# Relative-position attention: far value products in pairs every second step, six probability buffers, maxima respread

## The chip, the cores and the metric

One core of a Trainium2 chip runs the whole program. The metric is the device time of one execution in microseconds (us). Engines: TensorE (PE, matrix products; PEld is its weight load), VectorE (DVE), ScalarE (ACT), GpSimd (POOL), and SP, which issues DMA transfers.

## What is computed

A pre-norm transformer layer on x of 2 x 2048 x 256: attention with 16 heads of 16 and clipped relative positions (distance at most 64), then a feed-forward part with block-wise FP4 quantising (untouched here).

```python
dist = jnp.clip(idx[None, :] - idx[:, None], -R, R) + R          # R = 64
score = einsum('bhqd,bhkd->bhqk', q, k) + einsum('bhqd,qkd->bhqk', q, rel_emb_k[dist])
attn = softmax(score)
ctx = einsum('bhqk,bhkd->bhqd', attn, v) + einsum('bhqk,qkd->bhqd', attn, rel_emb_v[dist])
```

## The kernel before

`transformer_layer` runs projections, attention and the feed-forward part one after the other. Attention works in 32 iterations: 8 groups g (2 batch entries x 4 groups of 4 heads) times 4 query blocks qb of 512 queries. An iteration goes over all 2048 keys in 16 steps (STEPS). A step is one tile of 128 keys against 512 queries for 4 heads. Steps 0 and 1 hold the band of keys near the diagonal (`near_half`, L835), steps 2 to 15 the far ones (`far_half`, L859); steps 2 to 4 mix pieces of several tiles (`pieces`, L1137).

A step has two units, each of two heads. A unit is written by TensorE in two halves into two banks of psS. psS has four banks, so it holds two units: a unit's first half waits until ScalarE has read the unit two places before (`unit_free`, L831). ScalarE (`iteration`, L999) takes the exponential of each unit, 128 x 1024, into `band` or `probs`. `probs` (L596) has 4 unit buffers, which is two steps; before the first exp of a far step ScalarE waits on the semaphore pv_done until the value products that read those buffers are over (L1014 to L1017).

The order on TensorE is written out by hand: `ORDER` (L549) has one string per step, and the loop at L912 issues one piece of work per letter:

- S: half a unit of scores (L867; in steps 0 and 1 L847 and L854).
- M: one maximum product (L756), a 128 x 512 tile of scores of the coming query block into one of two banks of psA, from which VectorE takes the row maximum (`take`, L1044, L1047). Of an iteration's 64 products, each waits until the maximum two places before is taken (L754). They belong to the next iteration up to step 12, and from step 13 (ASTEPS) on to the one after it.
- V: in steps 3 to 15 the value products of the step before (`far_values`, L773 to L782): for each piece four products of 32 (or 17) columns of the array, one per head, from `probs` into psC. In step 0 it is those of step 15 of the previous iteration; in step 2 the band's own (`band_values`, L872).
- R: the relative products of the next block (L769), in steps 4 to 7; they use psS as a unit does, and ScalarE copies them to rel_scores (`copy_rel`, L990), VectorE reduces them (`rel_maxima`, L1049).
- P: positions (`positions`, L884, L896), 64 columns wide. F: `fold_positions` (L902, L909), 32 columns wide, into psC.
- D and B: denominators and their turning back (L789, L799) for the iteration before. T: the turn of the negated maxima (`turn_maxima`, L784), which wait for VectorE's minus maxima (L1055) in step 13; ScalarE copies them (L985), POOL cuts them in three parts (L699), SP stores them as query rows (L641), and the first near scores of the next iteration wait for that (L850).

VectorE (`iteration`, L1076) walks the same steps: `RATE[step]`, the count of M in a step's string, sets how many maxima it takes there, with the row maxima of R behind the third take of steps 5 to 8, the masks of positions ahead of steps 10 and 12, the reciprocal ahead of step 2 and the product behind the first take of step 3.

The semaphore pv_done is raised once per far value step, 14 in an iteration (VALUE_STEPS), and by 2 at the start; `copy_context` (L978) waits for all of an iteration's. ScalarE does it behind the second exp of the next iteration. In the last iteration (`ends`) there are no M, R and T, and the value products left over come behind the loop (L947).

Of the kernel before, what the change touches and what calls it, by code (L numbers as in the profile page):

```python
# [27 lines left out]
ACT = mybir.ActivationFunctionType  # L28
AX = mybir.AxisListType

P = 128
# [7 lines left out]
NQ = 512  # L39
# [463 lines left out]
class Consts:  # L503
# [20 lines left out]
STEPS = 16  # L524
# [10 lines left out]
VALUE_STEPS = STEPS - BAND_STEPS  # L535
# [11 lines left out]
PSTEP = 8  # L547

ORDER = (  # L549
    "SMSMVMSMSMMM", "SMSMMSMMSMMD", "SMSMVMMBSSM", "SMSSMSVM",  # L550
    "SMSSMSMVRM", "SMSSMSVRM", "SMSSMSMVRM", "SMSSMSVRM",
    "SMSSMSMVMP", "SMSSMSMVMP", "SMSSMSMVFMP", "SMSSMSMVMP",
    "SMSSMSVMF", "SMSSMSVMT", "SMSSMSVM", "SMSSMSVM",
)
RATE = tuple(x.count("M") for x in ORDER)
ASTEPS = 13
AHEAD = sum(RATE[ASTEPS:])
assert sum(RATE) == ROUND


def place(n, ends=False):

    return n if ends else n + min(max(n // 2 - RSTEP, 0), RUNITS)


def rel_place(k):

    return 2 * (RSTEP + k) + 2 + k


def first_of(it):

    return it * SEQ + RUNITS


def attention(nc, c, dr, io):
    with ExitStack() as ctx:
        def sb(name, shape, dt=F32):
            return ctx.enter_context(nc.sbuf_tensor(name, shape, dt))
# [13 lines left out]
        keys, qs, vals, keys_in, q_in = io.keys, io.qs, io.vals, io.keys_in, io.q_in  # L593
        rel = sb("rel_scores", [P, APAIRS, DREL])
        near = sb("rel_near", [P, APAIRS, 2, P])
        probs = sb("probs", [P, 4, 2, NQ])  # L596
        band = sb("band_probs", [P, 2, HG, CH, P])
        relp = sb("rel_products", [P, 2, NQ])
        amax = sb("amax", [P, APAIRS, APER])
# [139 lines left out]
        def _(pe):  # L739
# [33 lines left out]
            def far_values(g, qb, step, ends=False):  # L773

                pe.wait_ge(unit_done, first_of(g * QB + qb) + place(2 * step + 1, ends) + 1 + 2)
                for o, tile, q0, k in pieces(qb, step):
                    for h in range(HG):
                        n = 2 * step + h // 2
                        v = values_of(g, tile, h)
                        ins = t.matmul(psC[32 * h:32 * h + v.shape[1], q0:q0 + k], v,  # L780
                                       probs[:, n % 4, h % 2, o:o + k], start=False, stop=False, skip_group_check=True)
                ins.then_inc(pv_done, 1)  # L782

            def turn_maxima(m):  # L784
# [22 lines left out]
            def iteration(g, par, qb, gp, first=False, last=False):  # L807
                it = g * QB + qb
                base = first_of(it)
                ends = last and qb == QB - 1  # L810
                g1, par1, qb1 = (g + 1, 1 - par, 0) if qb == QB - 1 else (g, par, qb + 1)
                g2, par2, qb2 = (g, par, qb + 2) if qb < 2 else (g + 1, 1 - par, qb - 2)
                qp = (qb - 1) % QB

                todo = [] if ends else [(qb1, x) for x in maxima(g1, par1, qb1)][AHEAD:]
                ahead = [] if last and qb >= QB - 2 else [(qb2, x) for x in maxima(g2, par2, qb2)][:AHEAD]

# [94 lines left out]
                for step in range(STEPS):  # L912
                    if step == ASTEPS:
                        start_ahead()
                    score = near_half if step < BAND_STEPS else far_half
                    half = 0
                    for kind in ORDER[step]:
                        if kind == "M":
                            some(1)
                        elif kind == "S":  # L920
                            score(2 * step + half // 2, half % 2)
                            half += 1
                        elif kind == "R":
                            if not ends:
                                k = step - RSTEP
                                rel_products(it + 1, qb1, k, base + rel_place(k))
                        elif kind == "P":
                            positions(*divmod(step - PSTEP, 2))
                        elif kind == "F":
                            fold_positions((step - PSTEP) // 2 - 1)  # L930
                        elif kind == "D":
                            if not first:
                                denominators(it - 1)
                        elif kind == "B":
                            if not first:
                                turn_back(it - 1)
                        elif kind == "T":
                            if not ends:
                                turn_maxima(it + 1)
                        elif step == 0:  # L940
                            if not first:
                                far_values(gp, qp, STEPS - 1)
                        elif step == 2:
                            band_values()
                        else:
                            far_values(g, qb, step - 1, ends)
                if ends:  # L947
                    far_values(g, qb, STEPS - 1, ends)
                    denominators(it)
                    turn_back(it)  # L950

            pe.sem_inc(pv_done, 2)
            pe.wait_ge(keys_in, KDMAS * 16)
            pe.wait_ge(q_in[0], 6 * 16)
            for k in range(RUNITS):
# [3 lines left out]
            pe.wait_ge(q_in[1], 6 * 16)  # L959
            for item in list(maxima(0, 0, 1))[:AHEAD]:  # L960
                max_product(1, item)
# [12 lines left out]
        @block.scalar  # L974
        def _(act):
            a = nc.scalar

            def copy_context(it):  # L978


                act.wait_ge(pv_done, (it + 1) * VALUE_STEPS + 2)
                act.wait_ge(norm_ready, it + 1)
                a.copy(ctxs[:], psC[:]).then_inc(ctx_copied, 1)

            def copy_shift(m):  # L985

                act.wait_ge(turn_ready, m + 1)
                a.copy(sres[:, 0, :], psM[0:2 * APAIRS, 0:P]).then_inc(shift_copied, 1)  # L988

            def copy_rel(m, k, at):  # L990

                if k == 0:
                    act.wait_ge(skew_out, m * 16)
                act.wait_ge(rel_max, m * RUNITS)
                act.wait_ge(unit_ready, at + 1)
                a.copy(rel[:, 4 * k:4 * k + 4, :].rearrange("p (b x) r -> p b (x r)", b=2),  # L996
                       psS[:, 2 * (k % 2):2 * (k % 2) + 2, :]).then_inc(unit_done, 1)

            def iteration(g, qb, first=False, last=False):  # L999
                it = g * QB + qb  # L1000
                base = first_of(it)
                ends = last and qb == QB - 1
                for n in range(UNITS):
                    if n == 2 * ASTEPS + 2 and not ends:
                        copy_shift(it + 1)
                    if n == 2 and not first:
                        copy_context(it - 1)
                    act.wait_ge(unit_ready, base + place(n, ends) + 1)
                    src = psS[:, 2 * (place(n, ends) % 2):2 * (place(n, ends) % 2) + 2, :]
                    if n < 2 * BAND_STEPS:  # L1010
                        e, c2 = divmod(n, 2)
                        ins = a.activation(band[:, e, 2 * c2:2 * c2 + 2].rearrange("p h u q -> p h (u q)"), src, ACT.Exp)  # L1012
                    else:
                        if n % 2 == 0:  # L1014

                            act.wait_ge(pv_done, it * VALUE_STEPS + n // 2 - BAND_STEPS + 1)
                        ins = a.activation(probs[:, n % 4], src, ACT.Exp)  # L1017
                    ins.then_inc(unit_done, 1)
                    if n % 2 == 1 and RSTEP <= n // 2 < RSTEP + RUNITS and not ends:
                        k = n // 2 - RSTEP  # L1020
                        copy_rel(it + 1, k, base + rel_place(k))
                if ends:
                    copy_context(it)

            act.sem_inc(unit_done, 2)
            act.sem_inc(ctx_copied, 1)
            for k in range(RUNITS):
                copy_rel(0, k, k)
            copy_shift(0)
            iteration(0, 0, first=True)  # L1030
            for g in range(GRP - 1):
                for qb in range(1, QB):
                    iteration(g, qb)
                if g < GRP - 2:
                    iteration(g + 1, 0)
            for qb in range(QB):
                iteration(GRP - 1, qb, last=True)
# [3 lines left out]
        def _(dve):  # L1041
# [34 lines left out]
            def iteration(g, qb, first=False, last=False):  # L1076
# [3 lines left out]
                g1, qb1 = (g + 1, 0) if qb == QB - 1 else (g, qb + 1)  # L1080
                todo = [] if ends else [((it + 1) * ROUND, n) for n in range(AHEAD, ROUND)]
                ahead = [] if last and qb >= QB - 2 else [((it + 2) * ROUND, n) for n in range(AHEAD)]

# [7 lines left out]
                for step in range(STEPS):  # L1091
                    if step == ASTEPS:
                        assert not todo
# [30 lines left out]
            dve.wait_ge(negm_ready, 1)  # L1124
            for n in range(AHEAD):
                take(ROUND, n)
# [599 lines left out]
```

## Time and profile before

| | us |
|---|---|
| median of 3 runs (2590.91 to 2592.51) | 2591.05 |
| the profiled execution's own time | 2594.04 |
| its span, first to last instruction | 2592.3 |
| TensorE busy (share of the span) | 2382.4 (92%) |
| VectorE busy | 1930.2 (74%) |
| ScalarE busy | 1361.9 (53%) |
| POOL busy | 606.9 (23%) |

Mean granted clock of TensorE 0.972 (1.00 is the higher of its two levels, 2.4 GHz). Busy times overlap, and the ends of matmuls are modelled: a 512-column product counts 0.38 us while the next one can start after 0.22. Attention lies between about 180 and 2146 us of the span.

### The profile page before, as it was taken

The page shows a single profiled execution, that of the slowest core. Times are in us where ns is not written, and L with a number is a line of the kernel's source. Part 1 is how long each engine was busy: PE and PEld are TensorE (multiplying, and loading weights), DVE is VectorE, ACT ScalarE, POOL GpSimd, SP SyncE. Part 2 cuts the span into 40 slices and gives each one's busy share as a digit, 9 for nine tenths or more (in the row PEclk, how much of TensorE's full clock was granted, in tenths as well). Part 3 has the DMA queues.
Part 4 walks back from the last instruction along what each step waited for, and adds up shares of the span by engine and source line. Part 5 has one row for each costly group of instructions (what it writes and reads, how often), then busy time and mean ns, then how long its engine had stood idle before and what let it go on. Part 6 is the DMA issues. An engine that isn't in the chain of part 4 may idle for free. (4 is left out here: it accounts for less than half of the span.)

```text
span 2592.3 us, 47776 instructions
## 1 busy us (share of the span) xinstructions
PE 2382.4 (92%) x19372; PEld 1179.2 (45%) x19372; DVE 1930.2 (74%) x3509; ACT 1361.9 (53%) x1572; POOL 606.9 (23%) x361
## 2 busy tenths in 40 slices
PE   7879999999999999999999999999999993899997
PEld 3424444444444444444444444444444442566665
DVE  6587777777777777777777777777777726899997
ACT  3405555565555555555555555555555561334442
POOL 5402222222222222222222222222222220011111
PEclk9959999999999999999999999999999996999998
DMA  5723323332333333323332332333222221111110
GB/s 159 184 75 86 85 77 85 88 85 76 85 84 96 93 89 101 99 78 85 85 85 82 93 85 77 85 88 85 76 77 77 71 70 54 43 40 49 49 40 27
DMA packets 275656, 210.35 MB, mean 81 GB/s; under 512 B 17058, under 2 KB 266628, under 8 KB 275332
## 3 DMA queue, kind: packets, MB, share of 16 engines
q1 hardware_dynamic: 274308, 203.37, 28.5%
q0 software_dynamic: 1152, 4.19, 0.6%
q8 instruction: 144, 2.36, 0.4%
q14 instruction: 52, 0.43, 0.1%
HBM read 113.35 MB, written 93.34 MB: 80 GB/s over the span
## 5 line engine op out<-in xcount | busy, mean ns | idle before, releaser
L1047 DVE TENSOR_REDUCE amax<-psA 128x1 f32<-128x512 f32 x2048 | 1327.7, 686 | 494.3 <-PE psA L756 485.9
L1017 ACT ACTIVATE probs<-psS 128x1024 f32<-128x1024 f32 x896 | 885.0, 1023 | 483.5 <-PE psS L867 483.0
L756 PE MATMUL psA<-keys,queries 96*128 96x512 bf16 x2048 | 789.0, 392 | 43.8 <-DVE amax L1047 43.6
L867 PE MATMUL psS<-queries,keys 102*128 102x512 bf16 (+7 forms) x2176 | 632.5, 343 | 44.7 <-ACT rel_scores L996 36.8
L780 PE MATMUL psC<-probs,vals 128*32 128x512 f32 (+7 forms) x4352 | 475.0, 524 | 0.6 <-ACT probs L1017 0.6
L756 PEld LDWEIGHTS psA<-keys,queries 96*128 96x128 bf16 x2048 | 196.4, 97 | 500.5 <-DVE amax L1047 439.2
L717 POOL TENSOR_TENSOR band_probs<-band_probs,side 128x2048 f32<-128x2048 f32 x64 | 288.6, 4533 | 559.5 <-PE psC L880 559.5
L867 PEld LDWEIGHTS psS<-queries,keys 102*128 102x128 bf16 (+1 forms) x2176 | 203.4, 99 | 282.0 <-ACT rel_scores L996 98.1
L1012 ACT ACTIVATE band_probs<-psS 128x1024 f32<-128x1024 f32 x128 | 131.1, 1024 | 224.1 <-PE psS L854 224.1
L996 ACT COPY rel_scores<-psS 128x1024 f32<-128x1024 f32 x128 | 129.3, 1012 | 106.9 <-PE psS L769 106.9
L780 PEld LDWEIGHTS psC<-probs,vals 128*32 128x32 f32 (+1 forms) x4352 | 89.1, 102 | 174.0 <-issue 166.5
L1342 PE MATMUL psG<-w_gate_up_T,f_xqT 128*128 128x352 f32 x512 | 162.8, 473 | 0.9 <-ACT f_xqT L1396 0.9
L847 PE MATMUL psS<-ident,rel_near 128*128 128x128 f32 x1024 | 156.0, 274 | 0.0
L723 POOL TENSOR_TENSOR band_probs<-band_probs 128x2048 f32<-128x2048 f32 x32 | 145.0, 4531 | 5.7 <-POOL band_probs L721 2.9
L847 PEld LDWEIGHTS psS<-ident,rel_near 128*128 128x128 f32 x1024 | 129.6, 142 | 21.4 <-issue 2.0
L703 POOL CAST shift<-shift_res 32x128 bf16<-32x128 f32 x32 | 9.0, 281 | 520.0 <-ACT shift_res L988 520.0
L1281 POOL TENSOR_TENSOR f_hq<-f_h_grid,f_h_scale 128x704 f32<-128x704 f32 x32 | 44.4, 1387 | 355.2 <-DVE f_h_grid L1510 355.2
L1342 PEld LDWEIGHTS psG<-w_gate_up_T,f_xqT 128*128 128x128 f32 x512 | 97.7, 196 | 51.8 <-issue 4.9
L854 PE MATMUL psS<-queries,keys 102*128 102x128 bf16 (+1 forms) x1024 | 100.6, 220 | 6.7 <-DMA queries<-shift 6.7
L697 POOL MEMSET rel_near<- 128x256 f32 x16 | 5.1, 318 | 410.3 <-DMA rel_near<-rel_skew 410.3
L1374 PE MATMUL psD<-w_down_T,f_hqT 128*128 128x256 f32 (+1 forms) x384 | 96.5, 394 | 2.0 <-ACT f_hqT L1402 2.0
L1052 DVE TENSOR_REDUCE rel_max_of<-rel_scores 128x4 f32<-128x512 f32 x128 | 86.6, 676 | 10.2 <-ACT rel_scores L996 10.2
(162 smaller groups left out, 2054.2 us busy)
## 6 DMA issues: line engine op xcount, KB each, us to landing
rel_skew<-rel_scores SPq DMA_DIRECT2D x32, 2048.0 KB, 7.5
rel_near<-rel_skew SPq DMA_DIRECT2D x64, 1024.0 KB, 8.1
keys<-k_ring SPq DMA_DIRECT2D x48, 256.0 KB, 5.7
queries<-q_parts SPq DMA_DIRECT2D x192, 64.0 KB, 2.4
ctx_d<-rden SPq DMA_DIRECT2D x32, 256.0 KB, 2.3
ctx_in<-ctx_d SPq DMA_DIRECT2D x32, 256.0 KB, 2.7
q_parts<-parts SPq DMA_DIRECT2D x16, 384.0 KB, 2.9
k_ring<-parts SPq DMA_DIRECT2D x12, 384.0 KB, 3.1
```

The lines of the kernel that those rows point to most:

```text
L717: p.tensor_mul(both, both, c.side[:, e, None, :].broadcast_to([P, APAIRS, P])).then_inc(side_cut, 1)
L723: p.tensor_add(band[:, 0].rearrange("p h u q -> p (h u q)"), band[:, 0].rearrange("p h u q -> p (h u q)"), band[:, 1].rearrange("p h u q - ...
L756: t.matmul(psA[:, n % 2, :], qs[0:NR, qb, h, u * P:(u + 1) * P], keys[0:NR, par, h, c0:c0 + NQ], start=True, stop=True).then_inc(max_ready, 1)
L780: ins = t.matmul(psC[32 * h:32 * h + v.shape[1], q0:q0 + k], v, probs[:, n % 4, h % 2, o:o + k], start=False, stop=False, skip_group_check ...
L847: t.matmul(bank[:, u * P:(u + 1) * P], near[:, h * CH + u, e, :], c.ident[:], start=(u == 0), stop=False, is_transpose=True, skip_group_ch ...
L854: ins = t.matmul(bank[:, u * P:(u + 1) * P], keys[0:nr, par, h, c0:c0 + P], qs[0:nr, qb, h, u * P:(u + 1) * P], start=False, stop=(u == CH ...
L867: ins = t.matmul(bank[:, o:o + k], keys[0:nr, par, h, c0:c0 + P], qs[0:nr, qb, h, q0:q0 + k], start=True, stop=True, skip_group_check=True)
L996: a.copy(rel[:, 4 * k:4 * k + 4, :].rearrange("p (b x) r -> p b (x r)", b=2), psS[:, 2 * (k % 2):2 * (k % 2) + 2, :]).then_inc(unit_done, 1)
L1012: ins = a.activation(band[:, e, 2 * c2:2 * c2 + 2].rearrange("p h u q -> p h (u q)"), src, ACT.Exp)
L1017: ins = a.activation(probs[:, n % 4], src, ACT.Exp)
L1047: v.reduce_max(amax[:, pair, k:k + 1], psA[:, n % 2, :], AX.X).then_inc(max_taken, 1)
L1342: ins = t.matmul(psG[:, half, 0:GU], xqT[:, k, cc, :], wgu[:, cc, half * GU:(half + 1) * GU], start=(cc == 0), stop=(cc == 1))
```

## The change

`ORDER` is written anew. The value products of two far steps stand together in every even step but step 2, which keeps the band's: step s runs those of s-2 and s-1, and step 0 those of steps 14 and 15 of the previous iteration. Odd steps have none. The maxima per step go from 7 7 5 3 4 3 4 3 4 4 4 4 3 3 3 3 to 6 4 4 3 5 3 5 3 5 3 5 3 5 3 4 3, 64 in all as before, with the last three steps holding 9 before and 10 now. `probs` gets 6 unit buffers (three steps), the waits on pv_done count from 3 in place of 2, and `far_values` finds its buffers modulo 6. F of step 12 moves from behind an M to directly behind the couple; T still ends step 13.

```diff
--- before.py
+++ after.py
@@ -547,13 +547,15 @@
 PSTEP = 8
 
 ORDER = (
-    "SMSMVMSMSMMM", "SMSMMSMMSMMD", "SMSMVMMBSSM", "SMSSMSVM",
-    "SMSSMSMVRM", "SMSSMSVRM", "SMSSMSMVRM", "SMSSMSVRM",
-    "SMSSMSMVMP", "SMSSMSMVMP", "SMSSMSMVFMP", "SMSSMSMVMP",
-    "SMSSMSVMF", "SMSSMSVMT", "SMSSMSVM", "SMSSMSVM",
+    "SMSMVVMSMSMM", "SMSMSMSMD", "SMSMVMBSSM", "SMSSMSM",
+    "SMSMSMSVVMRM", "SMSSMSRM", "SMSMSMSVVMRM", "SMSSMSRM",
+    "SMSMSMSVVMPM", "SMSSMSMP", "SMSMSMSVVFMPM", "SMSSMSMP",
+    "SMSMSMSVVFMM", "SMSSMSMT", "SMSMSSMVVM", "SMSSMSM",
 )
 RATE = tuple(x.count("M") for x in ORDER)
 ASTEPS = 13
+
+PSTEPS = 3
 AHEAD = sum(RATE[ASTEPS:])
 assert sum(RATE) == ROUND
 
@@ -593,7 +595,7 @@
         keys, qs, vals, keys_in, q_in = io.keys, io.qs, io.vals, io.keys_in, io.q_in
         rel = sb("rel_scores", [P, APAIRS, DREL])
         near = sb("rel_near", [P, APAIRS, 2, P])
-        probs = sb("probs", [P, 4, 2, NQ])
+        probs = sb("probs", [P, 2 * PSTEPS, 2, NQ])
         band = sb("band_probs", [P, 2, HG, CH, P])
         relp = sb("rel_products", [P, 2, NQ])
         amax = sb("amax", [P, APAIRS, APER])
@@ -778,7 +780,7 @@
                         n = 2 * step + h // 2
                         v = values_of(g, tile, h)
                         ins = t.matmul(psC[32 * h:32 * h + v.shape[1], q0:q0 + k], v,
-                                       probs[:, n % 4, h % 2, o:o + k], start=False, stop=False, skip_group_check=True)
+                                       probs[:, n % (2 * PSTEPS), h % 2, o:o + k], start=False, stop=False, skip_group_check=True)
                 ins.then_inc(pv_done, 1)
 
             def turn_maxima(m):
@@ -913,7 +915,7 @@
                     if step == ASTEPS:
                         start_ahead()
                     score = near_half if step < BAND_STEPS else far_half
-                    half = 0
+                    half, values = 0, 0
                     for kind in ORDER[step]:
                         if kind == "M":
                             some(1)
@@ -937,19 +939,21 @@
                         elif kind == "T":
                             if not ends:
                                 turn_maxima(it + 1)
-                        elif step == 0:
-                            if not first:
-                                far_values(gp, qp, STEPS - 1)
                         elif step == 2:
                             band_values()
                         else:
-                            far_values(g, qb, step - 1, ends)
+                            back, values = 2 - values, values + 1
+                            if step:
+                                far_values(g, qb, step - back, ends)
+                            elif not first:
+                                far_values(gp, qp, STEPS - back)
                 if ends:
-                    far_values(g, qb, STEPS - 1, ends)
+                    for back in (2, 1):
+                        far_values(g, qb, STEPS - back, ends)
                     denominators(it)
                     turn_back(it)
 
-            pe.sem_inc(pv_done, 2)
+            pe.sem_inc(pv_done, PSTEPS)
             pe.wait_ge(keys_in, KDMAS * 16)
             pe.wait_ge(q_in[0], 6 * 16)
             for k in range(RUNITS):
@@ -978,7 +982,7 @@
             def copy_context(it):
 
 
-                act.wait_ge(pv_done, (it + 1) * VALUE_STEPS + 2)
+                act.wait_ge(pv_done, (it + 1) * VALUE_STEPS + PSTEPS)
                 act.wait_ge(norm_ready, it + 1)
                 a.copy(ctxs[:], psC[:]).then_inc(ctx_copied, 1)
 
@@ -1014,7 +1018,7 @@
                         if n % 2 == 0:
 
                             act.wait_ge(pv_done, it * VALUE_STEPS + n // 2 - BAND_STEPS + 1)
-                        ins = a.activation(probs[:, n % 4], src, ACT.Exp)
+                        ins = a.activation(probs[:, n % (2 * PSTEPS)], src, ACT.Exp)
                     ins.then_inc(unit_done, 1)
                     if n % 2 == 1 and RSTEP <= n // 2 < RSTEP + RUNITS and not ends:
                         k = n // 2 - RSTEP
```

## Rows read from the trace of the kernel before

**Rows 1.** Windows: attention, last iteration, feed-forward (span; PE PEld DVE ACT POOL busy; clock; DMA; GB/s).

```profile
254.00:1063.00 809.00, 775.38 (x7191) 356.63 (x7191) 603.49 (x986) 472.42 (x499) 199.35 (x103) 1.00 0.32 87
2101.27:2142.81 41.54, 38.99 (x451) 17.56 (x449) 2.33 (x4) 31.18 (x33) 14.08 (x4) 1.00 0.03 7
2146.00:2592.00 446.00, 360.23 (x1452) 254.81 (x1452) 382.21 (x908) 156.11 (x266) 50.54 (x36) 0.92 0.14 44
```

**Rows 2.** Windows: one iteration, steps 6-7, steps 12-13, steps 0-1.

```profile
1001.31:1063.01 61.70, 59.17 (x551) 27.11 (x550) 45.96 (x76) 36.14 (x39) 14.95 (x7) 1.00 0.34 89
1015.53:1023.17 7.64, 6.85 (x40) 2.24 (x39) 5.65 (x9) 5.91 (x6) 1.68 (x1) 1.00 0.01 2
1039.02:1045.07 6.05, 6.05 (x51) 2.01 (x48) 4.46 (x10) 3.82 (x4) 0.00 (x0) 1.00 0.28 69
1050.38:1062.04 11.66, 10.96 (x95) 7.71 (x94) 9.45 (x15) 4.67 (x6) 0.00 (x0) 1.00 0.43 81
```

**Rows 3.** Waits of TensorE in that iteration: total us, times, longest.

```profile
PE psS L867 <- ACT rel_scores L996: 1.2, 4, 0.3
PE psA L756 <- DVE amax L1047: 1.1, 4, 0.5
```

**Rows 4.** Timeline, TensorE: start, length, line, operation, count [idle before <-releaser].

```profile
1016.63 0.39 PE L867 MATMUL psS<-queries,keys 102*128 102x512 bf16 x1 [0.29 <-ACT rel_scores L996]
...
1017.08 0.38 PE L867 MATMUL psS<-queries,keys 102*128 102x512 bf16 x1
1017.67 0.39 PE L756 MATMUL psA<-keys,queries 96*128 96x512 bf16 x1 [0.21 <-DVE amax L1047]
1017.99 1.07 PE L780 MATMUL psC<-probs,vals 128*32 128x512 f32 x8
1018.99 0.61 PE L769 MATMUL psS<-rel_rows,queries 96*128 96x256 bf16 x4
1019.43 0.38 PE L756 MATMUL psA<-keys,queries 96*128 96x512 bf16 x1
...
1042.77 0.60 PE L867 MATMUL psS<-queries,keys 99*128 99x512 bf16 x2
```

**Rows 5.** Timeline, ScalarE and VectorE, at the same times.

```profile
1015.57 1.01 ACT L996 COPY rel_scores<-psS 128x1024 f32<-128x1024 f32 x1 [0.58 <-PE psS L769]
1016.47 2.04 ACT L1017 ACTIVATE probs<-psS 128x1024 f32<-128x1024 f32 x2
1019.69 1.01 ACT L996 COPY rel_scores<-psS 128x1024 f32<-128x1024 f32 x1 [1.17 <-PE psS L769]
...
1043.19 1.02 ACT L1017 ACTIVATE probs<-psS 128x1024 f32<-128x1024 f32 x1 [1.36 <-PE psS L867]
...
1016.93 1.88 DVE L1047 TENSOR_REDUCE amax<-psA 128x1 f32<-128x512 f32 x3
...
1019.85 0.69 DVE L1047 TENSOR_REDUCE amax<-psA 128x1 f32<-128x512 f32 x1 [0.45 <-PE psA L756]
```

**Rows 6.** Timeline, TensorE: value step, fold, maximum, positions, scores.

```profile
1033.00 1.06 PE L780 MATMUL psC<-probs,vals 128*32 128x512 f32 x8
1033.88 0.62 PE L909 MATMUL psC<-rel_products,fold 128*32 128x128 f32 x16
1034.43 0.39 PE L756 MATMUL psA<-keys,queries 96*128 96x512 bf16 x1
1034.75 0.69 PE L896 MATMUL psM<-band_probs,tv 128*64 128x64 f32 x16
1035.37 0.39 PE L867 MATMUL psS<-queries,keys 102*128 102x512 bf16 x1
```

**Rows 7.** Timeline, VectorE: minus maxima in step 13.

```profile
1042.58 0.22 DVE L1059 TENSOR_REDUCE negm<-amax 128x16 f32<-128x64 f32 x1
...
1043.13 1.29 DVE L1047 TENSOR_REDUCE amax<-psA 128x1 f32<-128x512 f32 x2
```

**Rows 8.** Groups by line, TensorE: near scores behind the shifts' transfer.

```profile
L854 PE MATMUL psS<-queries,keys 102*128 102x128 bf16 (+1 forms) x1024 | 100.6, 220 | 6.7 <-DMA queries<-shift 6.7
```

## The prediction

> **What bounds the kernel now.** The page ranks the engines: TensorE is the fullest, VectorE next, ScalarE behind. By stage, attention runs with TensorE 96% busy and the granted clock at 1.00, the feed-forward part behind it at 81% [rows 1]. The change touches attention alone, 32 iterations, so the question is what ends last there. A steady iteration lasts 61.70 us, and the same view cut at the starts of steps gives it in pairs of steps [rows 2]. TensorE sets the pace, but not by its work alone: it waits for ScalarE to free a score buffer (psS holds two units) and for VectorE to free one of two maximum buffers (psA) [rows 3]. These rows understate the waits, since a matmul counts 0.38 us as busy while the next one starts 0.22 behind it. So I count from start to start.
>
> **Slots**, start to start, in us: a half unit of scores (S) and a maximum product (M) 0.22 each (0.45 for both), a relative product (R) 0.45, a far value step (V) ahead of a full-width product 1.00, an M ahead of V 0.32 [rows 4]; V ahead of the fold (F) 0.88, F ahead of M 0.55, the position products (P) ahead of S 0.62 [rows 6]. Entering the narrow (32- and 64-column) products thus costs 0.10 and leaving them 0.11; net of that V is 0.87, F 0.45, P 0.50. Summed over an iteration, work and switches are 56.8 us; the other 4.9 are waits.
>
> **What the change removes.** Fourteen far value steps, of which each stands alone, become seven couples: seven entries and exits go, 7 x 0.21 = 1.5 us. The F of step 12 joins a couple, another 0.21. That is 1.7 us an iteration, all on TensorE's path. V beside V isn't in this trace. Its nearest row is V beside F, both 32 columns wide; the bounds are 0.87 (no exit) and 1.00 (an exit all the same). I take 0.87.
> The counts are otherwise the same: 64 M, 14 V, 4 R, the same transfers, exps and maxima; SP's and POOL's orders aren't touched. Two more buffers of probabilities cost 8 KB a partition and no instruction. ScalarE's wait before the first exp of step s now asks for the values of step s-3 where it asked for those of s-2. In the new order they stand in step s-2 or s-1 at the latest, so no exp waits for them and nothing queues behind that wait; without the third pair of buffers it would bind.
> T, the turn of the maxima, still ends step 13. The scores behind its transfer wait 6.7 us in all now, 0.2 a round [rows 8]; the way from T to them grows by 0.4 by the table below, so about half of that wait, 0.1, goes.
>
> **What it adds: waits.** Two rules come out of the rows [rows 4, 5]. An exp starts 0.42 after the second half of its unit, lasts 1.02, and the buffer is free 0.06 later; the copy of R starts 0.70 after R, and the next exp 0.90 after that copy. A maximum is taken 0.42 after its M started, takes follow each other by 0.60, one lasts 0.69, and the M two places on may go 0.06 later. Worked through the new order from the first S of step 5, at 0: R of step 5 at 2.02, M 2.47, S of step 6 at 3.04 (0.35 of it behind exp 11), M 3.26, S 3.48, M 3.70, S 4.05 (0.13 behind the copy of R). VectorE still has the last maximum and the row maxima of step 5 ahead, so its takes for step 6 start at 4.08 and 4.68, and the third M waits 0.56, to 4.83. S 5.05, V 5.37, V 6.24, M 7.22, R 7.44, M 7.89, and step 7 starts at 8.11. There the second unit waits 0.39 for the copy of R, and R 0.26 for an exp. Step 8 starts at 11.15. The pair 6-7 lasts 8.11, against 7.64 before [rows 2]: its waits grow from 1.3 to 1.75, the switch gives 0.21 back, and one M came in. While both Vs run, 1.85 us, ScalarE and VectorE empty their two buffers and stand idle; between couples six units and eight maxima come as a burst.
> Steps 12 and 13: step 12 now ends V V F M M. Those two takes and the three operations of the minus maxima, 0.55 [rows 7], stand in a row on VectorE; the first M of step 13 waits 0.50 for a take, the third 0.70. Nothing waited here before.
> The same rules over all pairs, as work + switches + waits:
> 2-3: before 7.1 + 0.6 + 0.4 = 8.1, after 6.0 + 0.4 + 0.4 = 6.8 (a V went to step 4);
> 4-5: before 5.9 + 0.4 + 0.7 = 7.0, after 6.15 + 0.2 + 1.6 = 8.0;
> 6-7: before 7.6, after 8.1;
> 8-9: before 6.3 + 0.85 + 0.8 = 7.9, after 6.3 + 0.6 + 1.15 = 8.1;
> 10-11: before 6.7 + 0.85 + 0.2 = 7.8, after 6.7 + 0.6 + 0.6 = 7.9;
> 12-13: before 5.4 + 0.6 + 0 = 6.0, after 5.8 + 0.2 + 1.6 = 7.7;
> 14-15: before 4.8 + 0.4 + 0.1 = 5.3, after 5.0 + 0.2 + 0.4 = 5.7;
> 0-1: before 10.1 + 0.2 + 1.3 = 11.5, after 10.1 + 0.2 + 0.2 = 10.5 (four Ms fewer, one V more, and the Ms there wait up to 0.5 now [rows 3]).
> Before comes to 61.3, against 61.70, and 7.6, 6.0 and 11.5 against 7.64, 6.05 and 11.66 [rows 2]. After comes to 62.8. Waits grow by 3.1, switches shrink by 1.7: **+1.44 an iteration**. Moving one input at a time (the spacing of takes by 0.01, a latency by 0.03, a slot by 0.005, the exit by 0.03) moves that between 1.2 and 1.6.
> The last iteration has no maxima and no R. Its steps hold four S, V and P, and the new order puts eight S ahead of V V, through two buffers that empty in 2 x 1.02 a step. By the same rules such a pair grows by 0.8, and with the last couple outside the loop some 6 come on top of 41.5 [rows 1].
> **Sum:** 30 x (1.44 - 0.11) = 40, the last iteration 6, the first and the one before the last about 0: +46. The profiled execution took 2594.04 (span 2592.3), the median of the runs is 2591.05, 3 us lower; 2594 + 46 = 2640 there, and **2637 us** on the median.
>
> The Trainium skill, page "TensorEngine Tiling" (Performance Considerations, PSUM Bottleneck), states that tiling speeds TensorE up and leaves the emptying of PSUM as it was, which then can become the bottleneck. This speaks against the change, and the trace agrees in that the waits named above are for exactly that; the page gives no figure for it.
>
> **Rivals.**
> *Only the switches count* (0.07). The waits stay at 4.9 and an iteration falls to 60.0: 31 x 1.7 = 53 less, 2538 us. For it: ScalarE and VectorE are busy 36 and 46 of 61.7 us [rows 2]. Against: even so TensorE waits for both today, two buffers deep, and a couple doubles the stretch which they must bridge. The Trainium skill, page "TensorEngine Tiling" (Key Properties), states that changing the tiling mode drains the engine; the 0.10 and 0.11 agree, and by that rule alone the result would be this one.
> *Waits grow, but less* (0.13), by 1.0 to 2.2 an iteration, as bursts overlap better than the account has it: 31 x (1.0 - 1.7) = -22 to 31 x (2.2 - 1.7) + 4 = +19, so 2569 to 2610.
> *The clock falls* (0.05). TensorE's idle share in attention grows; the part behind, at 81%, shows a granted clock of 0.92 [rows 1]. If 2% of it went in attention, 31 x 1.25 = 39 more, 2676.
> *The wait for buffers binds* (0.02). If the first exp of a step needed the couple beside it, each couple would cost one exp, 7 x 1.02 x 31 = 220 more, 2857. The counts, as reckoned above, exclude it.
> My own forecast, 2610 to 2656, has the remaining 0.73.
>
> **How the numbers follow.** A measurement of this kernel tells 0.2%, 5 us, from no change. Slower by more: my forecast, the clock, the wait, and half of the second rival, 0.86. Within it 0.03. Faster: the first rival and the rest of the second, 0.11. The range leaves out the first rival, the faster part of the second and the two high ones: 2604 to 2656.
>
> **What would show it.** Right: steps 6-7 at 8.1, 12-13 at 7.7 with two waits for maxima in step 13, 2-3 at 6.8; V to V at 0.87; idle time before M about doubled, before S up by a third; no exp behind a V; the last iteration near 47. Wrong: the waits before M and S at their old size, V to V at 1.00, or a granted clock under 1.00 in attention.

## Result and the profile after

The changed kernel takes 2631.92 us (median of 4 runs, 2630.7 to 2634.69), the kernel before 2591.78 us beside it: 40 us more, a ratio of 1.0154 with a 95% interval of 1.0136 to 1.0171. The forecast was 2637 us, 46 more than before.

First the page of the changed kernel, busy times and the granted clock:

```profile
PE 2370.5 (90%) x19372; PEld 1178.0 (45%) x19372; DVE 1919.3 (73%) x3509; ACT 1368.1 (52%) x1572; POOL 606.5 (23%) x361
...
PEclk9959999999999999999999999999999996999999
```

TensorE is busy 12 us less than before, though the program is 40 us longer. The work shrank (the entries into narrow products and the exits from them), the idle time grew. The granted clock in attention is 1.00, as it was.

Windows of the changed kernel: attention, then one iteration cut at the starts of its steps (2-3, 4-5 and so on to 14-15, then 0-1), with the columns of [rows 1]:

```profile
254.00:1063.00 809.00, 757.23 (x7074) 347.64 (x7072) 586.48 (x967) 468.85 (x491) 199.20 (x103) 1.00 0.32 86
1013.06:1019.88 6.82, 6.59 (x121) 4.34 (x121) 4.09 (x8) 3.20 (x5) 3.69 (x1) 1.00 0.01 2
1019.88:1028.18 8.30, 7.42 (x61) 2.93 (x61) 5.88 (x11) 6.04 (x7) 8.12 (x3) 1.00 0.10 32
1028.18:1036.30 8.12, 7.13 (x49) 2.50 (x49) 6.31 (x11) 5.91 (x7) 1.73 (x1) 1.00 0.00 0
1036.30:1044.12 7.82, 7.33 (x64) 2.73 (x64) 6.48 (x11) 4.52 (x5) 0.00 (x0) 1.00 0.77 262
1044.12:1052.06 7.94, 7.74 (x84) 3.22 (x80) 5.57 (x10) 3.99 (x5) 0.00 (x0) 1.00 0.66 166
1052.06:1059.74 7.68, 6.52 (x54) 2.23 (x50) 5.46 (x12) 3.92 (x5) 0.00 (x0) 1.00 0.45 112
1059.74:1065.58 5.84, 5.84 (x33) 1.44 (x31) 4.35 (x8) 3.52 (x6) 1.40 (x4) 1.00 0.02 4
1065.58:1075.97 10.39, 10.39 (x100) 7.76 (x100) 7.41 (x12) 5.25 (x6) 0.00 (x0) 1.00 0.48 90
```

In attention TensorE is busy 93.6% (757 of 809), 95.8% before [rows 1], with the clock still at 1.00. In the kernel before, the windows of steps 4-5 and 8-9, which [rows 2] doesn't have, are:

```profile
1008.46:1015.53 7.07, 6.76 (x61) 3.04 (x60) 4.46 (x7) 4.89 (x5) 6.89 (x2) 1.00 0.12 37
1023.17:1031.22 8.05, 7.55 (x66) 2.71 (x64) 6.82 (x11) 4.89 (x5) 0.00 (x0) 1.00 0.75 256
```

Cut by pairs, in us, with the forecast beside them:

| steps | before | changed | forecast |
|---|---|---|---|
| 2-3 | 8.11 | 6.82 | 6.8 |
| 4-5 | 7.07 | 8.30 | 8.0 |
| 6-7 | 7.64 | 8.12 | 8.1 |
| 8-9 | 8.05 | 7.82 | 8.1 |
| 10-11 | 7.80 | 7.94 | 7.9 |
| 12-13 | 6.05 | 7.68 | 7.7 |
| 14-15 | 5.31 | 5.84 | 5.7 |
| 0-1 | 11.66 | 10.39 | 10.5 |
| sum | 61.69 | 62.91 | 62.8 |

Cut from one band value step (in step 2) to the next, the twenty-nine inner iterations differ by 35.3 us in all, 1.22 each. The last two add 6.5. The first one became 2.6 us shorter: its steps 0 and 1, which hold no value step of an earlier iteration and now four Ms fewer, fell from 19.7 to 16.3, and the stretch from its band value step to the next grew by 0.8. That makes 39.2 us for the 32 iterations. What stands ahead of them came out 0.9 longer and what stands behind, in the same code, 3.4 shorter in this pair of executions, so the two spans differ by 36.7 and the medians by 40.

Waits of TensorE in that iteration of the changed kernel (against [rows 3]):

```profile
PE psA L758 <- DVE amax L1051: 2.7, 7, 0.6
PE psS L869 <- ACT probs L1021: 0.6, 3, 0.2
PE psS L869 <- ACT rel_scores L1000: 0.4, 2, 0.2
```

The waits behind VectorE went from 4 to 7 and from 1.1 to 2.7 us. By these rows those for ScalarE did not grow. The same view over the stretch 254 to 1063 us, thirteen iterations:

```profile
PE psA L758 <- DVE amax L1051: 35.4, 91, 0.6
PE psS L869 <- ACT probs L1021: 8.0, 39, 0.2
PE psS L869 <- ACT rel_scores L1000: 5.8, 26, 0.5
```

Behind VectorE it is 35.4 us here and 15.2 in the kernel before, whose rows for this stretch stand with the experiments below.

The timeline of TensorE and of VectorE through step 6 of the changed kernel (against [rows 4, 5]):

```profile
1028.41 0.38 PE L758 MATMUL psA<-keys,queries 96*128 96x512 bf16 x1
1028.63 0.38 PE L869 MATMUL psS<-queries,keys 102*128 102x512 bf16 x1
1028.85 0.38 PE L758 MATMUL psA<-keys,queries 96*128 96x512 bf16 x1
1029.09 0.39 PE L869 MATMUL psS<-queries,keys 102*128 102x512 bf16 x1
1029.97 0.39 PE L758 MATMUL psA<-keys,queries 96*128 96x512 bf16 x1 [0.50 <-DVE amax L1051]
1030.20 0.38 PE L869 MATMUL psS<-queries,keys 102*128 102x512 bf16 x1
1030.51 1.93 PE L782 MATMUL psC<-probs,vals 128*32 128x384 f32 x24
1032.37 0.39 PE L758 MATMUL psA<-keys,queries 96*128 96x512 bf16 x1
...
1028.64 0.67 DVE L1056 TENSOR_REDUCE rel_max_of<-rel_scores 128x4 f32<-128x512 f32 x1
1029.23 1.88 DVE L1051 TENSOR_REDUCE amax<-psA 128x1 f32<-128x512 f32 x3
1031.03 0.67 DVE L1056 TENSOR_REDUCE rel_max_of<-rel_scores 128x4 f32<-128x512 f32 x1
1032.80 1.94 DVE L1051 TENSOR_REDUCE amax<-psA 128x1 f32<-128x512 f32 x3 [1.09 <-PE psA L758]
```

The third M starts at 1029.97. It follows an S of 1029.09, so without a wait it would have stood at 1029.31: it is 0.66 us late, of which the row shows 0.50 as idle time. VectorE took the row maxima of R at 1028.64 and so reached the first maximum of this step, whose M had started at 1028.41, only at 1029.23. That take ends at 1029.92. Then the couple runs from 1030.51 to the M at 1032.37, 1.86 us, and VectorE has nothing to do from 1031.70 to 1032.80, an idle time of 1.09.

Step 12 and 13 of the changed kernel, TensorE and VectorE:

```profile
1056.36 0.60 PE L758 MATMUL psA<-keys,queries 96*128 96x512 bf16 x2
...
1057.53 0.39 PE L758 MATMUL psA<-keys,queries 96*128 96x512 bf16 x1 [0.35 <-DVE amax L1051]
...
1059.40 0.39 PE L758 MATMUL psA<-keys,queries 96*128 96x512 bf16 x1 [0.61 <-DVE amax L1051]
1059.63 0.27 PE L789 MATMUL psM<-ident,negm 128*32 128x128 f32 x1
1059.74 0.38 PE L869 MATMUL psS<-queries,keys 99*128 99x512 bf16 x1
...
1056.78 1.29 DVE L1051 TENSOR_REDUCE amax<-psA 128x1 f32<-128x512 f32 x2 [2.12 <-PE psA L758]
1058.11 0.22 DVE L1063 TENSOR_REDUCE negm<-amax 128x16 f32<-128x64 f32 x1
...
1058.65 1.89 DVE L1051 TENSOR_REDUCE amax<-psA 128x1 f32<-128x512 f32 x3
```

Two Ms stand at 1056.36 (one row), their two takes at 1056.78, and the minus maxima behind them until the next take at 1058.65. The M of 1057.53 waited for a take and the M of 1059.40 for the next but one. In the kernel before, VectorE passed here with TensorE never idle (6.05 of 6.05 us busy [rows 2]).

### The profile page after: what moved, and what is told of

Read it like the earlier page. It is cut to its first block and busy times, and to the rows that moved or that the text cites. A ratio compares the mean times of both kernels' runs of the same rounds, so it can differ in the third digit from the quotient of the medians.

```text
span 2629.0 us, 47776 instructions
## 1 busy us (share of the span) xinstructions
PE 2370.5 (90%) x19372; PEld 1178.0 (45%) x19372; DVE 1919.3 (73%) x3509; ACT 1368.1 (52%) x1572; POOL 606.5 (23%) x361
## 5 line engine op out<-in xcount | busy, mean ns | idle before, releaser
L1051 DVE TENSOR_REDUCE amax<-psA 128x1 f32<-128x512 f32 x2048 | 1313.9, 685 | 539.9 <-PE psA L758 535.0
L1021 ACT ACTIVATE probs<-psS 128x1024 f32<-128x1024 f32 x896 | 894.9, 1023 | 569.5 <-PE psS L869 568.0
L869 PE MATMUL psS<-queries,keys 102*128 102x512 bf16 (+7 forms) x2176 | 648.9, 344 | 37.5 <-ACT probs L1021 23.8
L782 PE MATMUL psC<-probs,vals 128*32 128x512 f32 (+7 forms) x4352 | 430.4, 521 | 0.6 <-ACT probs L1021 0.6
L782 PEld LDWEIGHTS psC<-probs,vals 128*32 128x32 f32 (+1 forms) x4352 | 110.3, 103 | 208.9 <-issue 131.5
L849 PE MATMUL psS<-ident,rel_near 128*128 128x128 f32 x1024 | 157.1, 276 | 0.7 <-ACT probs L1021 0.7
L849 PEld LDWEIGHTS psS<-ident,rel_near 128*128 128x128 f32 x1024 | 126.7, 142 | 28.2 <-ACT probs L1021 9.9
```

The lines of the kernel that those rows point to most:

```text
L849: t.matmul(bank[:, u * P:(u + 1) * P], near[:, h * CH + u, e, :], c.ident[:], start=(u == 0), stop=False, is_transpose=True, skip_group_ch ...
L869: ins = t.matmul(bank[:, o:o + k], keys[0:nr, par, h, c0:c0 + P], qs[0:nr, qb, h, q0:q0 + k], start=True, stop=True, skip_group_check=True)
L1021: ins = a.activation(probs[:, n % (2 * PSTEPS)], src, ACT.Exp)
L1051: v.reduce_max(amax[:, pair, k:k + 1], psA[:, n % 2, :], AX.X).then_inc(max_taken, 1)
```

## The experiments

The readings below rest on the time between starts, as in the prediction. For one steady iteration of each trace (the eleventh) the table gives its length from one band value step to the next and the number of changes between full-width and narrow products (the one product of T, which shows no such cost, is left out). "Late" is what lies between two starts beyond the usual spacing of the same two kinds of product, from 0.04 us up, put down to the piece that started late; the usual spacing is taken low in the range of all traces, so these sums are good to about 0.2 us. Near scores are those of steps 0 and 1.

| kernel | iteration, us | changes of width | late far S and R | late M | late near scores |
|---|---|---|---|---|---|
| before | 61.69 | 42 | 2.2 | 2.6 | 0.1 |
| changed | 62.90 | 26 | 2.4 | 5.3 | 0.2 |
| couples alone (e2) | 63.01 | 28 | 3.3 | 4.0 | 0.5 |
| maxima alone (e3) | 62.09 | 40 | 1.2 | 4.4 | 0 |
| changed, none ending step 12 (e4) | 62.83 | 26 | 2.5 | 4.8 | 0.4 |
| before, short takes (e5) | 59.29 | 42 | 2.2 | 0.2 | 0.2 |
| changed, short takes (e6) | 58.71 | 26 | 3.0 | 0 | 0.7 |
| before, light (e7) | 58.87 | 42 | 1.8 | 0.2 | 0.2 |
| changed, light (e8) | 56.35 | 26 | 1.4 | 0 | 0.2 |
| single, reordered (e9) | 57.21 | 36 | 0 | 1.0 | 0 |
| couples, reordered (e10) | 57.48 | 32 | 0.2 | 1.3 | 0 |
| halves together (e11) | 61.10 | 42 | 0 | 4.4 | 0 |
| single, reordered again (e12) | 56.96 | 34 | 0.1 | 0.6 | 0 |

The theory: the couples save 1.7 us of switches an iteration and lose more in waits, because both reading engines work from two buffers each and run dry while a couple runs. The rivals: the new spread of the maxima does the harm, not the couples; V beside V saves nothing; the third pair of buffers costs something.

### The buffers alone

```diff
-        probs = sb("probs", [P, 4, 2, NQ])
+        probs = sb("probs", [P, 6, 2, NQ])
...
-                                       probs[:, n % 4, h % 2, o:o + k], ...
+                                       probs[:, n % 6, h % 2, o:o + k], ...
...
-            pe.sem_inc(pv_done, 2)
+            pe.sem_inc(pv_done, 3)
```

> The order of before, with probabilities of three steps held in place of two and the wait on pv_done counted accordingly. My theory: the third pair of buffers does nothing by itself, since no exp waits for a value step in the order of before: 2592 us, within 3. Rival (the larger buffer or the shifted wait costs or gains something of its own): more than 5 us off.

Measured: 2592.71 us, ratio 1.0002 (0.9993 to 1.0011). The buffers and the shifted wait are worth nothing either way in the order of before. The couples were not run with four buffers, so that they need the third pair stays the prediction's argument.

### The couples alone and the maxima alone

Couples, with before's counts of maxima:

```diff
...
-    "SMSSMSMVRM", "SMSSMSVRM", "SMSSMSMVRM", "SMSSMSVRM",
-    "SMSSMSMVMP", "SMSSMSMVMP", "SMSSMSMVFMP", "SMSSMSMVMP",
+    "SMSSMSMVVRM", "SMSSMSRM", "SMSSMSMVVRM", "SMSSMSRM",
+    "SMSSMSMVVMP", "SMSSMSMMP", "SMSSMSMVVFMP", "SMSSMSMMP",
...
```

> Couples and six buffers as changed, but as many maxima in each step as before (7 7 5 3 4 3 4 3 4 4 4 4 3 3 3 3). My theory: the couples themselves bring the waits, because scores and maxima come as a burst between them; by the two rules an iteration takes 62.7 us against 61.4 for before's order, so 30 x 1.3 and some 4 in the last iteration: 2635 us. Rival (the new spread of the maxima is the fault, and the couples pay): the waits stay as before and an iteration loses 1.7 us of switches: 2540 us.

Measured: 2636.58 us, ratio 1.0169 (1.0154 to 1.0185), 44 us above the kernel before beside it, where the whole change adds 40.

Single value steps, with the changed counts of maxima:

```diff
...
-    "SMSSMSMVRM", "SMSSMSVRM", "SMSSMSMVRM", "SMSSMSVRM",
+    "SMSMSMSVMRM", "SMSSMSVRM", "SMSMSMSVMRM", "SMSSMSVRM",
...
-    "SMSSMSVMF", "SMSSMSVMT", "SMSSMSVM", "SMSSMSVM",
+    "SMSMSMSVFMM", "SMSSMSVMT", "SMSMSSMVM", "SMSSMSVM",
...
```

> Value steps stand alone as before, four buffers, but the maxima are spread as in the change (6 4 4 3 5 3 5 3 5 3 5 3 5 3 4 3, two of them behind V in step 12). My theory: 61.8 us an iteration against 61.4, most of it in step 13: 2604 us. Rival (the spread is the fault): its whole growth of waits, 3.1 us an iteration, is here: 2685 us. Rival (the spread does nothing): 2592 us.

Measured: 2603.92 us, ratio 1.0038 (1.0025 to 1.0052). Each alone is slower than before, by 44 and by 11 us, and together they are 40: the new spread costs alone and helps the couples a little. The waits of TensorE over the same stretch, 254 to 1063 us, show which wait each brings. The kernel before:

```profile
PE psS L867 <- ACT rel_scores L996: 15.6, 52, 0.6
PE psA L756 <- DVE amax L1047: 15.2, 54, 0.5
PE psS L867 <- ACT probs L1017: 3.0, 13, 0.2
```

Couples alone:

```profile
PE psA L758 <- DVE amax L1051: 20.8, 65, 0.5
PE psS L869 <- ACT rel_scores L1000: 8.1, 26, 0.6
PE psS L869 <- ACT probs L1021: 8.0, 39, 0.2
```

Maxima alone:

```profile
PE psA L756 <- DVE amax L1047: 24.9, 65, 0.6
PE psS L867 <- ACT rel_scores L996: 5.8, 26, 0.5
PE psS L867 <- ACT probs L1017: 3.0, 13, 0.2
```

By these rows the couples bring the waits behind exps (3.0 to 8.0) and halve those behind the copy of R; both parts lengthen those for maxima. But idle time hides up to 0.16 us of each wait. From start to start the couples alone make far S and R 1.1 us an iteration later (2.2 to 3.3) and M 1.4 (2.6 to 4.0): they starve TensorE through both readers. The spread does its harm in M alone (2.6 to 4.4), while far S and R come 1.0 sooner.

### The maxima that end step 12

```diff
-    "SMSMVVMSMSMM", "SMSMSMSMD", "SMSMVMBSSM", "SMSSMSM",
+    "SMSMVVMSMSMMM", "SMSMSMMSMD", "SMSMVMBSSM", "SMSSMSM",
...
-    "SMSMSMSVVFMM", "SMSSMSMT", "SMSMSSMVVM", "SMSSMSM",
+    "SMSMSMSVVF", "SMSSMSMT", "SMSMSSMVVM", "SMSSMSM",
```

> The changed kernel with the two maxima behind V V F in step 12 moved to steps 0 and 1. The waits of 0.50 and 0.70 us in step 13 must go. My theory: they are partly paid elsewhere, since the scores then come sooner than ScalarE empties and the maxima wait in steps 0 and 1: 62.5 us an iteration in place of 62.76, so 8 us off the changed kernel, 2624 us. Rival (each wait is worth its own length): 1.2 x 30 = 36 off, 2596 us.

Measured: 2629.02 us, ratio to before 1.0142 (1.0126 to 1.0157), 3 to 4 us under the changed kernel where 8 were expected. Two Ms of step 13 that had been late by 0.5 and 0.8 us are late by 0.15 and 0.05. In their place an M of step 1 is 0.66 late, the S behind T 0.14 and the first near scores 0.19, and the inner iterations are 0.17 shorter on the mean. A wait's length is not its price.

### VectorE's part, then both engines' part

These four kernels leave part of the work out, to see what is paid for it. First VectorE reads 16 of the 512 columns of each maximum:

```diff
-                v.reduce_max(amax[:, pair, k:k + 1], psA[:, n % 2, :], AX.X).then_inc(max_taken, 1)
+                v.reduce_max(amax[:, pair, k:k + 1], psA[:, n % 2, 0:16], AX.X).then_inc(max_taken, 1)
```

> The order of before; VectorE takes each maximum over 16 of the 512 columns only (the rest of that reduction is left out), so that hardly anything waits for it. By the two rules an iteration falls from 61.4 to 59.2 us: 2592 - 31 x 2.2 = 2524 us. If waits for VectorE were hidden anyway: 2592.

Measured: 2497.47 us.

> The changed order, maxima taken over 16 of 512 columns as in the run beside it. By the two rules 58.8 us an iteration in place of 62.8, so the couples come out even or just ahead of the order of before under the same cut: 2632 - 31 x 3.9 = 2511 us, 5 to 15 under the run beside it. The waits for ScalarE remain (3.8 us an iteration against 2.3). Rival (the loss of the change doesn't come through VectorE): it stays 40 above the run beside it, 2565 us.

Measured: 2484.8 us (two runs of each, 2.4 us to either side here). Both fell further than expected by some 26 us, of which 20 lie ahead of the first band value step: the first round of maxima, which nothing covers, waits for its takes, and that step stands at 180 us where it was at 200. The order between the two is what counts: with VectorE's waits gone the changed order is 13 us ahead, where it was 40 behind. So waits for maxima make 53 us of the difference between the two orders. ScalarE still takes most of the gain: late far S and R stand at 3.0 in the changed order and at 2.2 in the other, late near scores at 0.7 and 0.2.

For the second pair each far exp is cut to 128 of its 1024 columns as well, and the buffers are zeroed once at the start:

```diff
-                        ins = a.activation(probs[:, n % 4], src, ACT.Exp)
+                        ins = a.activation(probs[:, n % 4, :, 0:64], psS[:, 2 * (place(n, ends) % 2):2 * (place(n, ends) % 2) + 2, 0:64], ACT.Exp)
...
+            v.memset(probs[:], 0.0).then_inc(probs_zero, 1)
```

> The order of before; maxima over 16 of 512 columns, and each far exp over 128 of its 1024 columns (the rest is left out; the buffers are zeroed once at the start). Waits for both engines nearly gone: 58.8 us an iteration, 2512 us.

Measured: 2489.84 us, 22 under the expected 2512, again mostly by the stretch ahead (186 us where 200 stood).

> The changed order with the same two cuts. With the waits gone the switches alone are left, and the change must win: 1.7 us of switches an iteration, and up to 0.6 of remaining waits for the copy of R: 56.4 to 57.1 us, so 53 to 73 us under the run beside it. Rival (V beside V costs as much as V alone): no gain, the two runs within 5 us.

Measured: 2413.99 us, 76 under the run beside it, 3 more than the highest value expected. This is the change's gain laid bare: 2.52 us an iteration, of which shorter remaining waits make 0.6 and 16 changes of width fewer the rest, some 1.85, or 0.115 each where the forecast had 0.106. From the pair with short takes to this one the changed order's lead grew from 13 to 76 us: in this order of cutting, 53 us pass through the maxima and 63 through the far exps. The timeline of TensorE in the light changed kernel, one couple with its neighbours:

```profile
1046.03 0.38 PE L869 MATMUL psS<-queries,keys 99*128 99x512 bf16 x1
1046.34 1.93 PE L782 MATMUL psC<-probs,vals 128*32 128x384 f32 x24
1048.20 0.39 PE L758 MATMUL psA<-keys,queries 96*128 96x512 bf16 x1
```

S to V is 0.31, the two Vs to the M behind them 1.86. A lone V with a full-width product behind it takes 1.00 [rows 4], so the second V adds 0.86. The rival that V beside V costs as much as V alone is out.

### Another order

The couples are one way to lower what TensorE spends; the waits, 4.9 us an iteration before, are the larger item. First only the score halves were moved together, from step 3 on:

```diff
...
-    "SMSSMSMVRM", "SMSSMSVRM", "SMSSMSMVRM", "SMSSMSVRM",
+    "MSSMSSMVRM", "MSSMSSVRM", "MSSMSSMVRM", "MSSMSSVRM",
...
```

> The order of before with as many maxima and value steps in each step, but from step 3 on the two score halves of a unit stand side by side (M S S M S S in place of S M S S M S). By the two rules the waits for ScalarE go (2.2 to 0) and those for VectorE grow in their place (2.8 to 4.6), because the maxima stay spread by 3 and 4 a step and by 7 in steps 0 and 1: 60.9 us an iteration, 2577 us. Rival (the order of halves alone makes the gain of the reordered kernel): 2465 us.

Measured: 2574.79 us, ratio 0.9928 (0.9912 to 0.9945). The waits of TensorE over the same stretch:

```profile
PE psA L756 <- DVE amax L1047: 18.9, 53, 0.5
```

Nothing is left behind ScalarE. Those behind VectorE grew from 15.2 to 18.9, and counted by starts from 2.6 to 4.4 an iteration, which gave back most of the 2.2 gained. Then order and spread together:

```diff
-    "SMSMVMSMSMMM", "SMSMMSMMSMMD", "SMSMVMMBSSM", "SMSSMSVM",
-    "SMSSMSMVRM", "SMSSMSVRM", "SMSSMSMVRM", "SMSSMSVRM",
-    "SMSSMSMVMP", "SMSSMSMVMP", "SMSSMSMVFMP", "SMSSMSMVMP",
-    "SMSSMSVMF", "SMSSMSVMT", "SMSSMSVM", "SMSSMSVM",
+    "MVMSMSMSMSMM", "SMSMSMSMMDM", "SSMSSMVB", "MSSSSMMV",
+    "MSSMMSSMRMV", "MSMSSSMVMR", "MSSMMSSMVMRM", "SMSMSSMVRMM",
+    "VMSSMSSMPM", "SMSSSPV", "MMVMSMSSFPMS", "SMSPMMSSVM",
+    "SMSSSMVF", "MSSMSTMSV", "MSSSMSMV", "MSSMSSMVM",
```

> Single value steps and four buffers as before, all switches paid, but the letters of each step in another order: the maxima stand in twos between pairs of score halves (M S S M M S S M R M V), so that a unit is finished at once and its exp starts early. Chosen by working the two rules over many orders. By them 57.0 us an iteration against 61.4, waits down from 4.9 to about 0.4: 30 x 4.4 = 133 off 2592, 2459 us. If the rules leave something out that such orders meet: between 2480 and 2592.

Measured: 2452.44 us, ratio 0.9468 (0.9452 to 0.9483): 137 us faster than the kernel before, which lay 40 under the changed one. Its window of one iteration, with the columns of [rows 1]:

```profile
998.53:1055.73 57.20, 56.89 (x550) 27.29 (x550) 46.23 (x76) 35.96 (x39) 15.28 (x8) 1.00 0.30 87
```

and a stretch of TensorE's timeline:

```profile
1011.05 0.38 PE L756 MATMUL psA<-keys,queries 96*128 96x512 bf16 x1
1011.27 0.60 PE L867 MATMUL psS<-queries,keys 102*128 102x512 bf16 x2
1011.70 0.90 PE L756 MATMUL psA<-keys,queries 96*128 96x512 bf16 x2
1012.44 0.60 PE L867 MATMUL psS<-queries,keys 102*128 102x512 bf16 x2
1012.88 0.38 PE L756 MATMUL psA<-keys,queries 96*128 96x512 bf16 x1
1013.19 1.07 PE L780 MATMUL psC<-probs,vals 128*32 128x512 f32 x8
1014.19 0.39 PE L756 MATMUL psA<-keys,queries 96*128 96x512 bf16 x1
```

Two halves in one row (x2, 0.60) are a unit finished at once, two maxima stand between two units. TensorE is busy 56.89 of 57.20 us. Of the 4.5 us an iteration, 3.9 are waits. The rest is switches: the expectation says that all of them are paid, but in this order some Vs stand beside P or F, and the trace has 36 changes of width where before had 42. The same for couples:

```diff
...
-    "SMSMSMSVVMRM", "SMSSMSRM", "SMSMSMSVVMRM", "SMSSMSRM",
+    "VMSSMMSSMRMV", "MSSMSSMMRM", "VMSSMSSMVMR", "MSSMMSSMR",
...
```

> Couples in even steps and six buffers, the two value steps of a couple set apart by maxima or scores where that saves a wait, and the same kind of order as in the run beside it. By the two rules 57.1 us an iteration: 2463 us, so the couples bring nothing beyond what the order brings. If a couple's switches were worth more than its waits: 1.7 x 31 = 53 under the run beside it.

Measured: 2469.33 us, ratio 0.9532 (0.9516 to 0.9548), 17 above the single order where 4 were expected. Here all seven couples are drawn apart, with scores, maxima or positions between their two Vs, so no V stands beside a V any more, and 32 changes of width against 36 remain. Between these two orders the couples brought nothing; whether another order with true couples would was not tried. The last is a second single order of the same kind, with steps such as "MSMSSSMPV" and "MSSMSSMVPF", in which V stands beside P or F:

> Single value steps, four buffers, another order of the same kind as the first reordered one, in which a value step stands directly beside the positions or the fold in steps 9 to 12 and so shares their entry or exit: by the two rules 56.4 us an iteration against 57.0, 2592 - 30 x 5.0 = 2442 us, 10 under the first reordered kernel. If the first was already at what the order can give: 2452.

Measured: 2452.47 us (2451.17 to 2458.05), not told apart from the first, and 10 us above what was expected. Its steady iteration is 0.25 us shorter in the trace (56.96 against 57.21) where 0.6 was expected, and the stretch between its last two band value steps is 3.4 longer.

## Why the prediction was right

The time fell inside the forecast's own range, 5 us under its number (40 more than before where 46 were forecast), and the sign came from the step that carried it, waits +3.1 against switches -1.7 an iteration.

**Slots and switches.** Right. The couple takes 1.86 us with M behind it, so V beside V is 0.86 to 0.87, the value taken and not 1.00. 42 changes of width became 26; at 0.106 each that is the 1.7 of the sum. The exit was put a little low: 1.00 for a lone V less 0.86 to 0.88 for one without an exit is 0.12 to 0.14, not 0.11.

**Waits.** Right in size and place. Worked through step 6, the forecast had the third M at 4.83, V at 5.37, the M behind the couple at 7.22, step 7 at 8.11 and step 8 at 11.15; the trace, on the same scale, has 4.83, 5.37, 7.23, 8.11 and 11.16. Steps 12-13 took 7.68 against 7.7, with the two waits in step 13 where they were put (0.50 and 0.70 forecast, 0.52 and 0.77 from start to start). The largest misses are steps 4-5 (0.3 short) and 8-9 (0.3 long), which cancel by luck. Counted from start to start, late Ms grew by 2.7 us, late far S and R by 0.1 and late near scores by 0.1, 3.0 in all beside the forecast's 3.1 (the rounded items of its own table of pairs add up to 2.9). With 1.75 off for the slots that makes the measured 1.22, for a forecast of 1.33; over 30 iterations that is 3 of the 6 us.

**"Idle time before S up by a third".** Wrong. In the stretch of thirteen iterations it fell, from 18.6 to 13.8 us; the idle time before M, said to double, went to 2.3 times. From start to start, late far S and R are 2.4 against 2.2, so they hardly moved. As the timeline of step 6 reads, an M that is late by VectorE gives ScalarE the time it needed, so the next S is not late as well. Two runs bear this out: with the takes short the changed order has 3.0 of late far S and R (in the order of before they stay at 2.2), and with the maxima alone respread they fell from 2.2 to 1.2 while late M rose.

**The turned maxima.** Right in size, but not by its reasoning. It took half of 6.7 us over 32 rounds; 5.0 of these 6.7 are one wait ahead of the first near scores, the same in both traces. The sum of all such waits fell by 1.0 only. From start to start, though, the scores behind the transfer came 0.1 us late in nearly every iteration before, which idle time doesn't show, and in no inner iteration now: the 0.1 came out by luck.

**The first iteration.** Forecast as about 0, it became 2.6 us shorter. Its steps 0 and 1 have four Ms fewer (0.9 us of slots), and with them went 1.6 us of late Ms and 0.9 of late scores; 0.8 came on top behind them. This term was left at nothing, and it is most of what remains of the 6 us.

**The last iteration.** Forecast as +6 with nothing for the one before it. From the band step of the last but one iteration to the last value step the trace shows 97.66 us against 91.17, 6.5 more, of which 2.6 lie in the first of the two stretches (56.51 to 59.13) and 3.9 in the second. The sum held; two fifths of it lie in another place than forecast.

**The rivals.** "Only the switches count" failed, since the waits did grow; it is what the light pair shows when reading costs little: 76 us in favour of the change. "Waits grow, but less" failed, since they grew by 3.0. The clock stayed at 1.00. In the trace no exp waits for a V, so the wait for buffers never bound, and six buffers alone changed nothing. The Trainium skill, page "TensorEngine Tiling" (Key Properties), states that changing the tiling mode drains the engine; the 0.10 to 0.14 us a change agree with it, though no run tried what causes them. The same page (Performance Considerations, PSUM Bottleneck) states that tiling leaves the emptying of PSUM as slow as it was, so that it may become the bottleneck. That agrees with what decided here: 53 us through the maxima, and 63 more through the far exps.

## What to carry to other kernels

Where one engine feeds two slower readers through two buffers each, a long piece that needs neither reader belongs in small portions between the short pieces; putting it together saves its switches, but while it runs the readers have only two buffers of work. Before changing what is issued, write out the order with start-to-start slots and the moments at which buffers come free: that account held within 0.6 us an iteration for every order and every cut tried here, and it found 137 us in a mere rearrangement. Finish a unit's halves at once so that its reader starts early, but spread the other reader's pieces anew with it: the halves alone gave 18 us. And judge a wait by removing it, since 1.2 us of them gave back only 0.2.

## What the runs showed of the hardware

A change between 128-column bf16 products and 32- or 64-column fp32 ones costs TensorE about 0.10 us on entry (0.31 to 0.32 from S or M to V, where 0.22 is usual) and 0.12 to 0.14 on exit, also in the light kernels. Whether the width or the data type makes it was not tried. T, a single product with 32 columns of weights in fp32, shows none of it: it starts 0.23 behind its M and the S behind it another 0.11 later (1059.40, 1059.63, 1059.74), and 0.11 is also the spacing of full-width 128-column fp32 products in this trace (L849). Up to 0.77 us more than usual between two starts, and twelve such delays of over 0.3 in an iteration, left the granted clock at 1.00. Takes of 128x512 from PSUM last 0.69 us each and follow each other by 0.60, exps of 128x1024 by 1.02, but the exp behind a plain copy already by 0.90 [rows 5].
